# Two-layer graph network: one marks matmul with a ReLU for the source match, and the message scatter in three bfloat16 parts

## The reference

```python
h = jnp.maximum(_layernorm(x, axis=-1), 0.0)
# layer 0
ea  = edge_attr_16 @ W_edge.T + b_edge
msg = relu(h[src] + ea)
agg = segment_sum(msg, dst, num_segments=6250)
t   = (h + agg) @ W1.T + b1
t   = gamma * (t - mean(t, 0)) * rsqrt(var(t, 0) + eps) + beta
x   = x + relu(t) @ W2.T + b2
# layer 1
h = jnp.maximum(_layernorm(x, axis=-1), 0.0)
Y = relu(concat([h[src], edge_attr_64]) @ M_W.T + M_b)
Z = segment_sum(Y, dst, num_segments=6250)
x = x + relu(concat([h, Z]) @ U_W.T + U_b)
```

## Time and profile before

| | |
|---|---|
| median of 3 runs | 5229.31 us (5225.77 to 5229.66) |
| profiled execution | 5240.01 us, span 5238.2 us |
| mean granted PE clock | 0.738 |
| PE, PEld, DVE, ACT, POOL busy | 67%, 57%, 42%, 29%, 30% |
| first layer's batches | about 100 to 3900 us |
| second layer's batches | about 4050 to 5200 us |

### The profile page before, as it was taken

One profiled execution on the slowest core, in us unless ns is written; L12 is line 12 of the kernel. 1 busy time (PEld: TensorE's weight loads), 2 busy tenths in 40 slices (PEclk: granted clock), 3 DMA queues, 4 the chain that ended last, 5 costly groups with the idle time before them and its releaser, 6 DMA issues.

```text
span 5238.2 us, 97613 instructions
## 1 busy us (share of the span) xinstructions
PE 3526.3 (67%) x36481; PEld 2982.6 (57%) x36481; DVE 2178.1 (42%) x3991; ACT 1542.0 (29%) x3339; POOL 1562.0 (30%) x1627
## 2 busy tenths in 40 slices
PE   3456666665566656665666566656565999999998
PEld 2445554554455545554555455545454888888887
DVE  5323332333233323332233223323335777777776
ACT  3222222222222222222222222212225555555554
POOL 3443334333443344334433443344330000000000
PEclk8666666666666666666666666666677999999999
DMA  6443444344433443444334433443332444344442
GB/s 180 107 124 103 107 118 120 108 106 118 126 107 101 117 126 103 105 118 125 113 96 119 123 112 96 117 126 106 103 78 51 78 77 75 70 74 77 77 76 54
DMA packets 914064, 539.25 MB, mean 103 GB/s; under 512 B 701164, under 2 KB 868064, under 8 KB 913880
## 3 DMA queue, kind: packets, MB, share of 16 engines
q1 hardware_dynamic: 862168, 428.75, 34.9%
q0 software_dynamic: 51584, 109.05, 6.4%
q10 hardware_dynamic: 256, 0.68, 0.0%
HBM read 245.68 MB, written 292.66 MB: 103 GB/s over the span
## 4 chain that ended last, share of the span: by engine, by line
PE 42%; another core or an unknown queue 26%; issue 15%; DVE 8%; ACT 5%; DMA 1%; DVEq 1%; ACTq 1%; SPq 0%; POOL 0%; POOLq 0%
PE ps_w L805 21%; PE ps_r L792 7%; PE ps_p L767 7%; PE ps_b L777 5%; DVE arena L1157 2%; ACT arena L607 2%; DVE counted L1066 2%; DVE arena L1153 1%; PE ps_p L753 1%; PE ps_w L814 1%; ACT side L591 1%; ACT acc L580 1%; ACT dst_rel L601 1%; DVE arena L1121 1%
## 5 line engine op out<-in xcount | busy, mean ns | idle before, releaser
L805 PE MATMUL ps_w<-arena 128*64 128x128 f32 x10400 | 1751.8, 316 | 789.4 <-issue 741.1
L493 POOL DMA_INDIRECT edge_store<-side,slot_idx x1612 | 1554.2, 964 | 2337.2 <-ACT side L594 1852.2
L805 PEld LDWEIGHTS ps_w<-arena 128*64 128x64 f32 x10400 | 1367.8, 159 | 1015.2 <-issue 919.9
L1121 DVE TENSOR_SCALAR arena<-arena,iota_p 125x512 bf16<-125x512 bf16 (+1 forms) x1352 | 467.2, 349 | 1852.0 <-ACT arena L607 1088.5
L792 PE MATMUL ps_r<-tab,arena 125*128 125x64 bf16 x15600 | 802.7, 203 | 396.1 <-issue 278.5
L1157 DVE TENSOR_TENSOR arena<-ps_c,dst_rel 128x1024 f32<-128x1024 f32 (+1 forms) x728 | 806.6, 1108 | 619.2 <-PE ps_w L805 460.2
L607 ACT ACTIVATE arena<-ps_b 125x512 bf16<-125x512 f32 (+1 forms) x1352 | 747.2, 576 | 1006.8 <-remote 774.8
L792 PEld LDWEIGHTS ps_r<-tab,arena 125*128 125x128 bf16 x15600 | 647.7, 104 | 622.3 <-issue 546.6
L637 ACT ACTIVATE arena<-arena 128x512 f32<-128x512 f32 (+1 forms) x728 | 425.4, 584 | 1908.3 <-PE ps_w L805 981.4
L777 PE MATMUL ps_b<-ident_b,marks_b 128*125 128x128 bf16 x5200 | 623.6, 253 | 205.9 <-ACT dst_rel L601 186.9
L767 PE MATMUL ps_p<-w_both,side 80*128 80x128 f32 x3224 | 605.0, 337 | 189.2 <-DVE counted L1066 118.4
(11 more groups left out here) (112 smaller groups left out, 609.5 us busy)
## 6 DMA issues: line engine op xcount, KB each, us to landing
edge_store<-zeros SPq DMA_DIRECT2D x52, 3300.0 KB
arena<-edge_store SPq DMA_DIRECT2D x104, 1650.0 KB, 9.7
side<-attr SPq DMA_DIRECT2D x156, 256.0 KB
edge_store<-side,slot_idx POOLq DMA_INDIRECT x1612
side<-attr SPq DMA_DIRECT2D x52, 224.0 KB
side<-attr SPq DMA_DIRECT2D x156, 64.0 KB
acc_kept_l<-acc SPq DMA_DIRECT2D x2, 1562.5 KB, 9.6
side<-attr SPq DMA_DIRECT2D x52, 56.0 KB
```

What stands on the lines that cost most here:

```text
L493: pool.indirect_dma_start(out=store, in_=stage[:, c, i, :], in_offset=None, out_offset=bass.IndirectOffsetOnAxis(ap=slot_idx[:, s, t + i:t ...
L805: last = pe.matmul(ps_sum, msg[:, slot, t, :], dst_match[:, slot, t, :], start=(u == 0 and t == 0), stop=(u == NU - 1 and t == nt - 1))
L1121: dve.tensor_scalar(src_match[0:NODE_P, slot, i % 2, 0:nt * P], spread_src[0:NODE_P, slot, i % 2, 0:nt * P], iota_p[0:NODE_P, 1:2], None, ...
```

## The change

**Sources.** An edge has four marks instead of two, all bfloat16: the source row s, its square rounded, the remainder of the square, and the destination less the batch's first. ACT copies them in one step (`read_marks`). In the first layer PE turns three of them (`turn_marks`) so that a bucket's slots lie side by side, ACT copies the result and stores it to a new DRAM buffer `mark_rows` (`store_row`), and loads it back as three long rows (`load_row`, by SP in the second layer). The spread is then one matmul of three rows against (2p, -1, -1): for row p it gives 2ps - s^2, and ACT's ReLU with the bias 1 - p^2 gives relu(1 - (p - s)^2), one where p = s and else zero. That replaces the copy and DVE's match.

**Messages.** ACT's ReLU writes the message in float32; DVE subtracts its upper half (the bfloat16 made of its upper 16 bits) and, in the first layer, does so again; in the second layer POOL does the second subtraction (`split_last`). The scatter reads the upper halves of the three parts as one moving side of 192 columns; the bfloat16 match of the destination is the stationary side. Its sum is 128 nodes by 3 x 64, which ACT copies (`copy_sum`) and PE turns back with three float32 matmuls that add the parts (`turn_sum`). The destination match is bfloat16, and its ramp lies in SBUF.

**Elsewhere.** Window starts are read from the first edge of each batch, in `destinations`, and `window_starts` is gone; `general_needed` takes the range check in its place. Several semaphores are merged.

```diff
 def spread_marks(layer, n, s, i):
     d, m, (j, nt) = dense_sems[layer], n * 2 + s, HALVES[i]
     if i == 0:
-        pe.wait_ge(d.meta_done, m * 2 + 2)
-    pe.wait_ge(d.copied, halves(m, i))
-    for t in range(nt):
-        last = pe.matmul(ps_b[(s + i) % 2][0:NODE_P, t * P:(t + 1) * P],
-                         marks_b[:, s, j + t:j + t + 1].broadcast_to([P, NODE_P]), ident_b[:, :],
-                         start=True, stop=True)
-    last.then_inc(d.bcast_done, 1)
+        pe.wait_ge(d.row_landed[s], n * 16 + 16)
+    pe.wait_ge(d.src_matched, halves(m, i))
+    pe.matmul(ps_b[(s + i) % 2][0:NODE_P, 0:nt * P], spread_w[D:D + PARTS, :], row_flat[:, s, j * P:(j + nt) * P],
+              start=True, stop=True).then_inc(d.spread_done, 1)
+
+def turn_marks(m, s):
+    pe.wait_ge(dense_sems[0].meta_done, m + 1)
+    for k in range(PARTS):
+        last = pe.matmul(ps_marks[:, k, :], marks_b[:, s, k, :], ident_b[:, :], start=True, stop=True)
+    last.then_inc(marks_turned, 1)
...
 def scatter(layer, m, s, u):
-    pe.wait_ge(d.relu_done, units(m, u) + 2)
+    pe.wait_ge(d.parts_done, units(m, u))
     pe.wait_ge(d.dst_matched, units(m, u))
...
     for t in range(nt):
-        last = pe.matmul(ps_sum, msg[:, slot, t, :], dst_match[:, slot, t, :],
+        last = pe.matmul(ps_sum, dst_match[:, slot, t, :], msg_upper[:, slot, t, :],
                          start=(u == 0 and t == 0), stop=(u == NU - 1 and t == nt - 1))
+
+def turn_sum(layer, m, s):
+    pe.wait_ge(d.sum_copied, m + 1)
+    pe.wait_ge(d.window_copied, m + 2)
+    for k in range(PARTS):
+        last = pe.matmul(ps_turned, group_sum[:, s, k * D:(k + 1) * D], prm("identity"),
+                         start=(k == 0), stop=(k == PARTS - 1))
...
-def copy_spread(layer, n, s, i):
+def match_src(layer, n, s, i):
...
-    act.activation(spread_src[...], ps_b[...], ACT.Copy).then_inc(d.copied, 1)
+    act.activation(src_match[...], ps_b[...], ACT.Relu, bias=one_less_square[0:NODE_P, 1:2]).then_inc(d.src_matched, 1)
...
+def store_row(n, s):
+    act.wait_ge(marks_turned, m + 1)
+    act.activation(turned_marks[:, s, :, :], ps_marks, ACT.Copy).then_inc(turned_copied, 1)
+    act.wait_ge(turned_copied, m + 1)
+    act.dma_start(mark_rows[bass.ds(m, 1)].rearrange("a k (j p) -> j (a k) p", p=P), turned_marks[:, s, :, :])
+
+def load_row(n, s):
+    act.wait_ge(row_stored[s], n * 16 + 16)
+    act.dma_start(row_flat[:, s, :], mark_rows[bass.ds(m, 1)].rearrange("a k n -> (a k) n"))
...
+def split(layer, m, s, u):          # VectorE
+    dve.wait_ge(d.relu_done, units(m, u) + 2)
+    dve.tensor_tensor(msg[:, slot, 0:nt, 1, :], msg[:, slot, 0:nt, 0, :], msg_upper[:, slot, 0:nt, 0:D], ALU.subtract)
+    if layer == 0:
+        dve.wait_ge(d.rest_split, units(m, u))
+        dve.tensor_tensor(msg[:, slot, 0:nt, 2, :], msg[:, slot, 0:nt, 1, :], msg_upper[:, slot, 0:nt, D:2 * D], ALU.subtract)
...
+def split_last(m, s, u):            # GpSimd, second layer
+    pool.wait_ge(d.rest_split, units(m, u))
+    pool.tensor_tensor(msg[:, slot, 0:nt, 2, :], msg[:, slot, 0:nt, 1, :], msg_upper[:, slot, 0:nt, D:2 * D], ALU.subtract)
...
-    dve.tensor_tensor(dst_match[:, slot, 0:nt, :], iota.unsqueeze(1).broadcast_to([P, nt, WINDOW]),
-                      dst_rel[:, s, j:j + nt].unsqueeze(2).broadcast_to([P, nt, WINDOW]), ALU.is_equal)
+    dve.tensor_tensor(dst_match[:, slot, 0:nt, :], iota_b[:, :].unsqueeze(1).broadcast_to([P, nt, WINDOW]),
+                      marks_b[:, s, 3, j:j + nt].unsqueeze(2).broadcast_to([P, nt, WINDOW]), ALU.is_equal)
```

More of the change, by code:

```diff
@@ L640, in dense @@
                         evacuate(m + 2, s, 2 * u - 3)
+                    if u == NU - 2 and not last:
+                        read_marks(layer, n + s, 1 - s)
+                    if u == NU - 1 and not last:
+                        if layer == 0:
+                            load_row(n + s, 1 - s)
+                        for i in range(2):
+                            match_src(layer, n + s, 1 - s, i)
                 if last:
+                    copy_sum(layer, m, s)
                     copy_window(layer, m, s)
@@ L817, in begin @@
             def begin(layer):
+                if layer == 0:
+                    turn_marks(0, 0)
                 for i in range(2):
@@ L833, in dense @@
                         project(m + 2, s, i - 5)
-                    if i == NH - 1 and not last:
-                        for k in range(2):
-                            spread_marks(layer, n + s, 1 - s, k)
+                    if i == NH - 1 and layer == 0 and not last:
+                        turn_marks(m + 1, 1 - s)
                     if i % 2 == 1 or i == NH - 1:
@@ L841, in dense @@
                             scatter(layer, m - 1, 1 - s, NU - 2 + u)
+                    if i == NH - 1 and not last:
+                        for k in range(2):
+                            spread_marks(layer, n + s, 1 - s, k)
+                    if i == 5 and not first:
+                        turn_sum(layer, m - 1, 1 - s)
                     if u == 3 and i % 2 == 1 and not first:
```

380 lines of the change are left out of this document (215 added, 165 removed).

## The result

The changed kernel takes 5352.6 us (median of 4; 5338.2 to 5358.8) where the kernel before took 5227.5 beside it: the ratio is 1.0235 (95%: 1.0214 to 1.0257), slower: outside the predicted range, and slower where faster was forecast. The profiled execution took 5350.2 us, its span 5348.4.

A forecast was written before the change was run, and what follows sets the result against it. First layer bound by GpSimd's scatter runs and, between them, a chain across engines; second layer by TensorE. Profiled 5240 - 175 (first layer) - 156 (second) = 4909, less 11 for the median: 4898 us; 8 in 10 between 4690 and 5130.

The forecast's parts named there:

- First layer, -3.5 a batch: First layer: cheaper scatter and spread, less added subtractions, save 3.5 us a batch, -175 us over 50 batches.
- forecast -0.5: First layer, stretch between GpSimd's two scatter runs in a batch: one cheaper scatter saves 0.5 us.
- forecast -3.0: First layer, stretch behind GpSimd's second run: -0.98 - 2.4 for scatters, -0.6 for spreads, +1.0 for subtractions.
- its cover: First layer: the marks' DRAM round trip costs nothing up to 19.4 us, hidden beside GpSimd's second run.
- TensorE falls to about 12.3 ... VectorE becomes the bound: Second layer: TensorE's busy time falls from 20.8 to about 12.3 us a batch; VectorE, at 16.2, sets the pace.
- The rival for it: Rival 3, second layer: TensorE, busy some 60%, drops to 1.2 GHz; 26.4 us a batch, total 5257; chance 0.09.
- The spread becomes at most 3: Second layer, TensorE: the spread falls from 5.2 to at most 3 us a batch.
- Half of GpSimd's time in VectorE's way: Second layer: half of GpSimd's 6.6 us subtraction time delays VectorE, adding 3.3 us to 16.2, giving 19.5 a batch.
- Rival 1: Second layer: VectorE and GpSimd exclude each other; 21.9 us a batch, total 5023; chance 0.25.
- the loop: Second layer: subtractions on VectorE and GpSimd, then scatter, fit within VectorE's 2.6 us of other work if nothing stretches.
- Head "within 5 us": Kernel's head: fewer reductions and transposes against a few small instructions, counted as nothing, within 5 us either way.
- the 16.2 us without waits: Second layer: VectorE's own work of 16.2 us a batch, the lower end if the engine loop fits.

The follow-up runs named there:

- a0: The changed kernel, run again unchanged: 5335 us, 1.022 of the kernel before; second layer 27.30 us a batch.
- b0: The kernel before the change, run again unchanged: 5215 us; second layer 22.57 us a batch at a clock of 1.00.
- e1: Changed kernel plus 14 unread matmuls of 500 columns in TensorE's wait at each second-layer batch's end: 4423 us, 1.225 of the kernel before beside it.
- g3: g2 with the last three second-layer scatters a step later and ACT matching the next batch's first sources before the last ReLU: 4904 us, ratio 0.939 to before.
- s1: The change's scatter part alone, with the spread of the kernel before (four matmuls, copy, match, no DRAM rows): 5204 us, ratio 0.998 to before.
- s2: The change's spread part alone, with the float32 scatter and match of before (ramp in SBUF), no subtractions: 5195 us, ratio 0.994 to before.
- c1: Changed kernel whose second-layer spread contracts 128 rows of constants instead of 3 rows (sums wrong): 5125 us, ratio 0.979 to before.
- c2: Changed kernel plus two unread matmuls of 500 columns behind each second-layer spread: 5344 us, ratio 1.021 to before.
- c4: c2 with the second-layer ramp of the destination match in PSUM, as in e3: 5188 us, ratio 0.991 to before.
- g2: Changed kernel, second-layer spread of 128 rows (125 zeros) and the destination match's ramp in PSUM: 4928 us, ratio 0.945 to before.
- e3: Changed kernel with the second-layer destination match's ramp in PSUM instead of SBUF: 4362 us, 1.205 of the kernel before beside it.

## Why the prediction was wrong, step by step

- **First layer, -3.5 a batch: right in size** (-3.2 in the profile, -2.9 in a0 against b0). By the starts of GpSimd's indirect DMAs (means over the layer) the pause between the two runs went from 7.3 to 5.7 us (forecast -0.5), the pause behind the second from 30.7 to 28.3 (forecast -3.0), and the runs themselves grew by 0.6. So the two places were right, and how the gain is shared between them was not. The row landed within its cover, as counted. Inside, scatters in the pause run at half clock and take 1.46 us, not 1.28, and the three turning matmuls of the sum, 1.54 us there (L886 at 2123.77), were not in the sum for this layer.
- **"TensorE falls to about 12.3 ... VectorE becomes the bound": the step that failed.** It took today's clock of 1.00 for given. TensorE is busy 22.9 us of the 27.3 (922.58 of 1100), and 17 of them go at half clock. The rival for it was there, with a batch of 26.4, but with a chance of 0.09, and its reason was another: it supposed TensorE busy 60%, and it was busy 84%. e1 and g3 show that this share does not tell: 96% busy at 0.69, 75% busy at 1.00. The idling that was named beside it is not needed either, as e1 shows. What the runs show in its place is that the two parts of the change lose the clock together (s1 0.81, s2 0.97, both 0.69), and that the spread's 3 rows have a large share in it (c1: 0.87).
- **"The spread becomes at most 3": mis-sized.** It was taken as about halved. With 128 rows and at full clock the one matmul a half still takes 5.0 us a batch (g3: 176.2 and 11.2 us in 37.3 batches) where four took 5.2, and with 3 rows it also holds up its neighbours: 0.81 us from gather to gather against 0.62 before. Times 12.5 that is an estimate of 2.4 us a batch more for TensorE at full clock, which had 1.7 us of idle time in a batch to take it in (20.9 of 22.57 busy in b0). In s2 a batch at full clock grew by 0.55.
- **"Half of GpSimd's time in VectorE's way", 3.3 us: near in size, by luck.** c2 to c4 measure 3.4, c1 to g2 3.45, but the 3.3 was the middle between nothing and never side by side, not a reading, and the clock moved in both pairs (0.87 to 0.95 and to 0.89). The exclusion that the Trainium skill's "SBUF — State Buffer" ("Who interferes with whom") states is what e3's durations show. As the clock had set the batch, it was not worth that here (e3: 0.9). Rival 1 put it at 21.9 a batch at a clock of 1.00; c1, which has the exclusion and a clock of 0.87, comes to 23.05.
- **The idle stretch at a batch's end** was not in the prediction at all: the loop was checked for full units and not for the last, of 2 tiles. With 128 rows and the ramp in PSUM it costs 0.8 us a batch, its share in the clock included (g2 to g3).
- **Head "within 5 us": 9.4.** The last two batches of the first layer, which have no run of GpSimd beside them, lost another 11 us (29.0 and 11.3 between weight matmuls became 36.6 and 15.0); the forecast left them at nothing.

Would the forecast have held at full clock? Not with this second layer. g3 comes to 18.79 a batch where 19.5 were forecast, and as a whole to 4904 where 4898 stood, but g3 has no exclusion, no wait for the last unit and 128 rows: the 16.2 us without waits were 2.6 too few, and the 3.3 for GpSimd stood in for them. The nearest to the change as written is c1, with 23.05 a batch (no gain over 22.57) and 5125 in all, 2% faster than before.

## What to carry to other kernels

Price TensorE's new work at both levels of the clock. Here a spread of 3 rows for one of 128 and a bfloat16 scatter for a float32 one left the engine looking nearly as busy (84% for 92%), and the granted clock alone showed the loss: look at it first, before the busy share. Check an engine chain also for the shortest unit and the end of a batch, and keep one operand of VectorE in PSUM where GpSimd works beside it. A DRAM round trip that is free because something else is slow is not free.
